# Where GpSimd multiplies a state's input by B, in a selective scan spread over five engines

## The reference

```
x_dbl = xm @ xp_w.T
delta = softplus(x_dbl[..., :64] @ dt_w.T + dt_b)
Bm, Cm = x_dbl[..., 64:80], x_dbl[..., 80:96]
A = -exp(A_log)
h = h * exp(d_t[:, :, None] * A) + (d_t * u_t)[:, :, None] * B_t[:, None, :]
y = einsum('bds,bs->bd', h, C_t)
```

## Time and profile before

| | |
|---|---|
| median of the timed runs | 3520.41 us |
| span of the profiled execution | 3546.8 us |
| TensorE busy | 2817.5 us (79%) |
| VectorE (DVE) busy | 2358.7 us (67%) |
| ScalarE (ACT) busy | 1928.5 us (54%) |
| GpSimd (POOL) busy | 1775.1 us (50%) |
| mean granted TensorE clock | 0.914 of full speed |

### The profile page before, as it was taken

How to read it: one execution, slowest core, us unless ns; L and a number is a source line. 1 busy time by engine, 2 the same in 40 slices (tenths; PEclk the granted TensorE clock), 3 DMA queues, 4 the chain that set the end, 5 groups by cost and what they waited for, 6 DMA issues and landing times.

```text
span 3546.8 us, 46325 instructions
## 1 busy us (share of the span) xinstructions
PE 2817.5 (79%) x15402; PEld 2084.2 (59%) x15403; DVE 2358.7 (67%) x3266; ACT 1928.5 (54%) x3239; POOL 1775.1 (50%) x1888
## 2 busy tenths in 40 slices
PE   3888788788887995788788788887996898999910
PEld 1666566666675653666566666675656665766600
DVE  3888988988882444888988988882444332333347
ACT  4877877887781324877887887771331111111100
POOL 1777767777781001777767777781100123222261
PEclk8998999999999896998999999999995799999955
DMA  3110111111111000011111111111102023122131
GB/s 107 31 36 32 34 36 34 34 36 41 40 44 55 28 9 25 31 37 32 35 34 34 34 37 39 40 46 54 36 1 86 33 79 132 49 77 78 50 96 55
DMA packets 101822, 163.32 MB, mean 46 GB/s; under 512 B 16610, under 2 KB 55778, under 8 KB 101634
## 3 DMA queue, kind: packets, MB, share of 16 engines
q1 hardware_dynamic: 80242, 109.94, 9.8%
q0 software_dynamic: 18064, 49.21, 4.1%
q10 hardware_dynamic: 3328, 1.76, 0.2%
HBM read 127.01 MB, written 24.38 MB: 43 GB/s over the span
## 4 chain that ended last, share of the span: by engine, by line
PE 42%; DVE 23%; ACT 13%; issue 11%; DMA 9%; POOL 1%; SPq 0%; another core or an unknown queue 0%; POOLq 0%; DVEq 0%; ACTq 0%
PE psD L1083 14%; DVE arena L1614 9%; PE psD L1181 6%; PE psA L1200 5%; ACT arena L931 4%; DMA write_w_sb<-x_dram,read_w_sb 4%; DMA write_w_sb<-write_w_sb 3%; ACT arena L921 3%; PE psD L1412 3%; DMA read_w_sb<-arena 2%; PE psD L1283 2%; PE psA L1083 2%; PE psA L1258 2%; PE psA L1190 2%; PE psD L1304 2%
## 5 line engine op out<-in xcount | busy, mean ns | idle before, releaser
L720 POOL TENSOR_TENSOR arena<-arena 128x512 f32<-128x512 f32 x1024 | 1154.2, 1154 | 17.8 <-DVE arena L1614 7.4
L1181 PE MATMUL psD<-ident,arena 128*128 128x128 f32 x4096 | 686.7, 293 | 344.4 <-DVE arena L1614 318.3
L1181 PEld LDWEIGHTS psD<-ident,arena 128*128 128x128 f32 x4096 | 482.3, 148 | 605.2 <-DVE arena L1614 375.8
L931 ACT ACTIVATE arena<-arena,negA 128x512 f32<-128x512 f32 x1024 | 719.2, 711 | 26.4 <-DVE arena L1614 25.7
L1614 DVE TENSOR_TENSOR_SCAN arena<-arena,carry,psD 128x512 f32<-128x512 f32 x512 | 641.9, 1269 | 83.3 <-PE psA L1200 75.2
L1614 DVE TENSOR_TENSOR_SCAN arena<-arena,psD 128x512 f32<-128x512 f32 x512 | 612.9, 1208 | 93.4 <-PE psA L1200 75.6
L1200 PE MATMUL psA<-ident,arena 128*128 128x128 f32 x4096 | 645.1, 283 | 0.0
L921 ACT ACTIVATE arena<-arena,bc 128x512 f32<-128x512 f32 x768 | 546.0, 711 | 118.3 <-PE psD L1181 117.6
L1200 PEld LDWEIGHTS psA<-ident,arena 128*128 128x128 f32 x4096 | 510.1, 148 | 2.1 <-issue 2.1
L704 POOL TENSOR_SCALAR arena<-arena,bc 128x512 f32<-128x512 f32 x256 | 180.8, 707 | 460.7 <-PE psD L1181 390.7
L1083 PE MATMUL psD<-arena 128*128 128x512 f32 (+4 forms) x776 | 336.1, 568 | 45.9 <-POOL strip L664 31.1
(11 more groups left out here) (230 smaller groups left out, 3840.8 us busy)
## 6 DMA issues: line engine op xcount, KB each, us to landing
arena<-c_dram SPq DMA_DIRECT2D x256, 256.0 KB, 3.1
arena<-in_W POOLq DMA_DIRECT2D x16, 1024.0 KB, 7.4
write_w_sb<-write_w_sb SPq DMA_DIRECT2D x72, 128.0 KB, 2.0
ys_dram<-arena POOLq DMA_DIRECT2D x70, 128.0 KB, 2.0
arena<-in_x SPq DMA_DIRECT2D x8, 1024.0 KB, 7.2
o_dram<-arena SPq DMA_DIRECT2D x32, 128.0 KB, 1.7
arena<-o_dram SPq DMA_DIRECT2D x4, 1024.0 KB, 5.4
x_dram<-arena SPq DMA_DIRECT2D x4, 1024.0 KB, 9.5
```

The costliest lines, as they stand in the source:

```text
L720: pool.tensor_tensor(h_ring[:, c % H_SLOTS, :], h_ring[:, c % H_SLOTS, :], c_rows[:, v % C_SLOTS, :], ALU.mult).then_inc(c_weighed, 1)
L931: act.activation(da_ring[:, c % DA_SLOTS, :], dt[:, i % 2, f, :], ACT.Exp, scale=negA[:, f, n:n + 1]).then_inc(da_ready, 1)
L1181: mm = pe.transpose(psD[:, c % FILL_BANKS, j * P:(j + 1) * P], g[:, (c // KI) % 2, j, c % KI * P:(c % KI + 1) * P], ident[:, :])
```

## The change

In GpSimd's loop the `spread_b` that stood ahead of the weighing now stands behind it, and is written for c+3 where it was written for c+6. In iterations c = 4m+1 the list is now: weigh chunk 4m-3, spread state m+1, then background work. Before, the spread between the same two weighings (4m-3 and 4m-2) was that of state m+2, and background work of iteration 4m+1 stood ahead of it. ScalarE's three tiles stay where they were, six chunks ahead. What a spread waits for is unchanged.

```
                     r, k, s, p, p2 = when(c)
-                    if (c + 6) % KI == 0 and 0 <= (c + 6) // KI < ITEMS * NS:
-                        spread_b((c + 6) // KI)
                     if 0 <= c - WEIGH_AFTER < RUN:
                         weigh_c(c - WEIGH_AFTER)
+                    if (c + 3) % KI == 0 and 0 <= (c + 3) // KI < ITEMS * NS:
+                        spread_b((c + 3) // KI)
```

## The result

The changed kernel takes 3490.95 us (median of 4 runs, 3486.49 to 3495.93), the kernel before, on the same chip, 3518.28 us (4 runs, 3515.83 to 3524.91). The ratio is 0.9923, interval 0.9906 to 0.994: 27 us faster. I had forecast no change that could be told (3521 us) and a range down to 3495.

The account below looks back on a forecast made before the run. VectorE, 88% busy in the recurrence, was taken as nearest to a bound, reached by GpSimd's order only through 125.7 us of waits. Terms +4 - 8 + 5 = +1 us on 3520.4 gave 3521 us; 8-in-10 range 3495 to 3552.

Parts of the forecast that it names:

- the openings: Start of a stretch: the same neighbours stay beside VectorE's small halo sums, so the change gains or costs nothing there.
- the waits of the overlap: VectorE instructions waiting on GpSimd: second halves +4 us, first halves -8, line 1572 +5, sum +1 us.
- the 125.7 us: VectorE's durations above their least: 114.2 us on five softplus lines and 11.5 us on line 1572.
- the wait that goes: GpSimd's 390.7 us idle at its spread for `fill`; waits move to the weighing, worth nothing on the path.
- rival B: Set up with the experiments: weighings come earlier and something depending on them (`add_y`, loads of C) gains; no chance given.
- The spread in time: In first halves the spread takes about 3.4 us against three scans' 3.62 us, so `fill` is not delayed; cost nothing.
- the 0.2 us: Margin by which the spread of first halves was said to be ready before `fill` needs it.
- the cover that the prediction named: In first halves, background work on VectorE lengthens most chunks, and with them the spread's margin before `fill`.
- The walk through the overlap: Hand-walked order of VectorE and GpSimd: waits +0.7 us per second half, -1.0 per first half; line 1572 +0.8 per second half.
- the tail of each burst: First halves: end of GpSimd's run of copy, four weighings and spread, said to cost VectorE 1.6 us a stretch.
- rival one: VectorE wins at scan ends, only spreads and softens cost: 45 us saved, 3475 us, softplus sum near 70; chance 0.23.
- The sign that I gave for being wrong: If the time moves but the softplus lines' mean-minus-least sums do not, another engine is behind it; no size given.

Follow-up runs that it names:

- the second halves' 7 us: The kernel before with the spread's new place in second halves of sequences alone, the old place in first halves: 3516.52 us, ratio 0.9975, 7 us faster.

## Why the prediction was wrong

Three terms failed: the openings (nothing was said, 7.2 us measured), the waits of the overlap (+1 us said, -13.3 measured), and TensorE's lower clock behind such waits, which was left out.

*What bounds the kernel: right in the main.* GpSimd reaches the bound through VectorE's durations; without contention in the softplus 107 us of the recurrence are gone. But the 125.7 us were not "the only way in which GpSimd's order reaches the bound": the halo sums were not counted among them.

*"Worth on the path: nothing"* for the wait that goes: it holds as far as semaphores go, since rival B fell. But this wait decided when the weighings began. The copy now waits for its scan, and a weighing begins in the mean 5.6 us behind its scan in first halves (7.2 before) and 1.6 us in second halves (7.0; the last stretch of a group is left out).

*The spread in time: right in cost, not in the 0.2 us.* I said that `fill` would have no wait for line 704. TensorE's idle time before `fill` after (us, times):

```profile
  DVE arena L1614: 662.7, 850
...
  POOL arena L704: 6.7, 9
```

Six of the nine are ties with a scan (0.01 us), but in all eight first halves the spread of the state that begins at chunk 48, behind two softens, does end late, 0.49 us behind the scan that `fill` waits for. Such a place (start us, duration us):

```profile
291.14 1.21 DVE L1614 TENSOR_TENSOR_SCAN arena<-arena,psD 128x512 f32<-128x512 f32 x1
...
292.15 0.69 POOL L704 TENSOR_SCALAR arena<-arena,bc 128x512 f32<-128x512 f32 x1
...
292.27 1.11 DVE L1587 SCALAR_TENSOR_TENSOR arena<-arena 128x512 f32<-128x512 f32 x1
...
292.94 0.63 PE L1181 MATMUL psD<-ident,arena 128*128 128x128 f32 x4 [0.72 <-POOL arena L704]
...
293.30 1.21 DVE L1614 TENSOR_TENSOR_SCAN arena<-arena,psD 128x512 f32<-128x512 f32 x1
```

The scan of two chunks earlier ended at 292.35; `fill` began only when the spread was through. It costs nothing: VectorE is in line 1587 until 293.38 and then in the scan of the chunk between, and the scan that reads this bank begins only at 295.15. That is the cover that the prediction named.

*"At the opening of a stretch the same neighbours stay beside VectorE's small halo sums: nothing": wrong.* This is the first step that failed. The neighbours are the same, their order is not, and `add_bias` is a piece of 2.4 us that VectorE must sit out. The new order gave 7 us, in the mean of two executions, of which a part is the clock; with `add_bias` moved away the openings had 15.9 us to give.

*The walk through the overlap: right in its kind, wrong in its sizes.* First halves: -1.0 us of waits in each was said, -1.6 measured in the softplus (7.97 to 6.34), and -0.5 on line 1572 (1.22 to 0.69), for which I had put down nothing there. I had the tail of each burst meet VectorE (1.6); after, the products of line 1603 (chunks 43, 44, 54 and 55) waited 0.17 us instead of 1.92, of which chunks 54 and 55 make 0.11 instead of 0.93. Second halves: +0.7 said, -0.6 measured (7.90 to 7.34). There line 1582 (chunks 30 to 36) waited 0.01 us instead of 2.12, 0.86 of it at chunk 32, where a soften had been in front of it; other lines took back 1.5. Line 1572 in second halves: +0.8 said, +1.2 measured (0.29 to 1.50), and its median over all stretches went from 256 ns to

```profile
L1572 DVE TENSOR_TENSOR arena<-arena,halo_sum x64: 161/352/840, 47.6 to 2176.8; 128x3 f32<-128x3 f32 x64
```

In sum +1 us was said and -13 came. The sum of 97.9 us lies between the forecast's 114 and the 70 that rival one named: this rival came in by less than half.

*A term that was missing.* I counted a wait as its own length and no more. A wait of VectorE can let TensorE idle too, and the transposes that follow may run at the lower clock: 2.1 us in one opening. The granted clock of 0.95 stood in the earlier trace rows, and the prediction made nothing of it. The sign that I gave for being wrong (time moves, these sums do not) came half true: 13 us from the sums, the rest from the openings and from TensorE.

**Open:** the second halves' 7 us; what makes the slow transposes of one kernel vary by 100; and some 4 us of the softplus, after 17 to 20 us of waits and 98 slow transposes at 40 ns (4 us); why the clock falls behind one stall and not behind an equal one.

## What to carry to other kernels

When an instruction moves in an engine's order, look at every stage in which it has new neighbours, and at short ones too: a 0.7 us piece in front of a 2.4 us piece was enough to let the other engine slip ahead of it. Price a wait by what it starts as well as by its length, above all where TensorE idles behind it and its granted clock falls. And a walk through overlaps tells where waits appear and go, but its sum over 14 stretches was off by 14 us, half of the whole effect: an error of 1 us in each stretch is enough for that.

## What the hardware showed beyond what I expected

The price of a short stall was not its length, and not a fixed one. In stretch 1 TensorE idled 3.2 us before the change; that was followed by 7.3 us at a granted clock of 0.54 in the first execution, and by none in group 1 of the second. After the change it idled 2.4 us; three of four openings kept the clock at 1.00, one did not. The length alone does not decide: with the spread behind the weighing but six ahead, a stall of 2.2 us was followed by the lower clock in all four openings of stretches 1 and 2. With TensorE at work through the stall (20 transposes in 2.35 us) the clock stayed at 1.00. The Trainium skill, "TensorE: Matmul & The Clock Gate", Part 1, tells of a clock that is low by default and that activity raises, which agrees with these rows as far as they go. It also puts the ramp's price at under 1% of a typical span; no run here measures what the lower clock costs this kernel in all.
